# A Mamba and mixture-of-experts layer on one core: the places of all steps in a 64-slot timetable are renumbered

## What is computed

```python
x = L0_attn_x                                   # (8, 1024, 512)
xz = layernorm(x) @ in_proj_w.T                 # x_ssm and z
x_conv = silu(causal_conv4(x_ssm) + conv_b)
B, C, delta = split(x_conv @ x_proj_w.T)        # 16, 16 and 1 wide; softplus on delta
def step(h, inp):                               # scan over 1024 steps, state 512 x 16
    h = exp(dt * A) * h + dt * B * xt
    return h, (h * C).sum(-1)
y = (ys + D_param * x_conv) * silu(z)
x = x + y @ out_proj_w.T
p = softmax(layernorm(x) @ router_w.T + router_b)
w, idx = top_k(p, 2)                            # two of eight experts per token
x = x + sum_k w_k * (layernorm(x) @ expert_weights[idx_k])
```

## Time and profile before

| what | value |
|---|---|
| time, median of 3 runs | 2778.48 us (2769.5 to 2797.36) |
| profiled execution, its own time | 2768.58 us |
| its span, first to last instruction | 2766.5 us, mean granted clock 0.926 |
| busy of the span | PE 84%, DVE 82%, POOL 65%, ACT 54% |
| instructions | 34600 |

### The profile page before, as it was taken

How to read it: one execution, slowest core, us unless ns; L and a number is a source line. 1 busy time by engine, 2 the same in 40 slices (tenths; PEclk the granted TensorE clock), 3 DMA queues, 4 the chain that set the end, 5 groups by cost and what they waited for, 6 DMA issues and landing times.

```text
span 2766.5 us, 34600 instructions
## 1 busy us (share of the span) xinstructions
PE 2313.6 (84%) x9510; PEld 1336.4 (48%) x9510; DVE 2273.5 (82%) x3144; ACT 1488.8 (54%) x2417; POOL 1809.8 (65%) x1418
## 2 busy tenths in 40 slices
PE   5668777798979889798988889798987989798886
PEld 2435353554545454454545455454544545454432
DVE  3899999899899989898999979898899989888200
ACT  3554646465654746565564656556574656545221
POOL 2556767557576767768676766767686676669442
PEclk8878788799989999898999989899999999999998
DMA  3873412324233434435343444534444353456875
GB/s 121 277 264 95 155 59 58 96 77 134 73 122 112 138 118 116 132 111 145 114 146 103 123 132 109 145 104 148 115 121 128 105 155 107 126 153 183 217 209 152
DMA packets 192570, 366.27 MB, mean 132 GB/s; under 512 B 22912, under 2 KB 22912, under 8 KB 192384
## 3 DMA queue, kind: packets, MB, share of 16 engines
q1 hardware_dynamic: 144272, 263.26, 29.8%
q0 software_dynamic: 28672, 67.13, 11.3%
q10 hardware_dynamic: 19440, 33.69, 3.4%
HBM read 212.73 MB, written 151.26 MB: 132 GB/s over the span
## 4 chain that ended last, share of the span: by engine, by line
PE 33%; DVE 24%; POOL 15%; issue 14%; ACT 11%; DMA 2%; SPq 0%; DVEq 0%; POOLq 0%; another core or an unknown queue 0%; ACTq 0%
DVE h L1069 13%; PE bank L1240 12%; PE bank L1244 11%; POOL u L785 9%; PE bank L1255 7%; DVE acc L1077 6%; ACT bank L930 4%; PE bank L1235 3%; DVE xc L1100 2%; ACT L930 1%; ACT xc L982 1%; POOL row_scratch L872 1%; PE bank L1317 1%; POOL row_scratch L870 1%; POOL x_out L885 1%
## 5 line engine op out<-in xcount | busy, mean ns | idle before, releaser
L785 POOL TENSOR_TENSOR u<-xc,b_ring 128x1024 f32<-128x1024 f32 x512 | 1230.2, 2419 | 644.4 <-DVE h L1069 434.9
L930 ACT ACTIVATE bank<-dt,neg_a 128x512 f32<-128x512 f32 x1024 | 701.6, 689 | 799.4 <-DVE h L1069 686.4
L1255 PE MATMUL bank<-ident,h 128*128 128x128 f32 x4096 | 643.4, 292 | 240.5 <-DVE h L1069 137.5
L1255 PEld LDWEIGHTS bank<-ident,h 128*128 128x128 f32 x4096 | 511.2, 150 | 559.4 <-DVE h L1069 206.2
L1069 DVE TENSOR_TENSOR_SCAN h<-bank,h_last,u 128x512 f32<-128x512 f32 x512 | 652.7, 1276 | 93.8 <-ACT bank L930 52.6
L1077 DVE SCALAR_TENSOR_TENSOR acc<-bank,ct,acc 128x512 f32<-128x512 f32 x960 | 696.5, 726 | 7.7 <-PE bank L1255 7.5
L1069 DVE TENSOR_TENSOR_SCAN h<-bank,u 128x512 f32<-128x512 f32 x512 | 620.9, 1215 | 92.8 <-ACT bank L930 54.6
L1240 PE MATMUL bank<-w_exp,xeT 128*128 x764 | 381.6, 623 | 43.5 <-ACT xeT L1038 20.5
L1244 PE MATMUL bank<-w_exp,xeT 128*128 x764 | 362.1, 596 | 0.0
L1240 PE MATMUL bank<-xnT,w_in 128*128 128x512 f32 x512 | 257.4, 627 | 9.2 <-DVE acc L1077 3.6
L1244 PE MATMUL bank<-xnT,w_in 128*128 128x512 f32 x512 | 242.3, 596 | 0.0
(11 more groups left out here) (149 smaller groups left out, 2193.1 us busy)
## 6 DMA issues: line engine op xcount, KB each, us to landing
b_ring<-b_scratch SPq DMA_DIRECT2D x256, 256.0 KB
xe<-row_scratch SPq DMA_DIRECT2D x165, 256.0 KB
result_scratch<-ye SPq DMA_DIRECT2D x165, 256.0 KB
row_scratch<-x_out ACTq DMA_DIRECT2D x32, 1024.0 KB, 5.4
x<-in_x SPq DMA_DIRECT2D x66, 256.0 KB, 4.3
x_scratch<-x SPq DMA_DIRECT2D x64, 256.0 KB, 2.4
xn<-in_x SPq DMA_DIRECT2D x62, 256.0 KB, 3.7
x_out<-x_scratch SPq DMA_DIRECT2D x44, 256.0 KB, 4.6
```

The source lines that it names most:

```text
L785: nc.gpsimd.tensor_tensor(out=u[:, at:at + 2, :], in0=xc[:, half, 2 * k:2 * k + 2, :], in1=b_ring[:, n % ROWS:n % ROWS + 1, :].to_broadcas ...
L930: nc.scalar.activation(decay_bank(j, n, c)[:], dt[:, half, :], ACT.Exp, scale=neg_a[:, c, n:n + 1]).then_inc(decay_ready, 1)
L1255: last = nc.tensor.transpose(ps[:, k * P:(k + 1) * P], tile(k), ident[:])
```

## The change

It gives every step of every table a new place. The steps themselves, their waits, the buffers and the number of banks stay. The diff is a list of numbers from end to end, of which two lines show the kind:

```diff
     POST = {
-        "y_gate": [6.67, 6.71, 10.4, 10.55],
+        "y_gate": [8.48, 9.55, 10, 11.25],
...
     EXPERTS = {
-        "rows_evict": [11.12, 15.78, 21.27, 24.77, 30.71, 34.35, 36.91, 44.06, 46.66, 53.82, 62.38, 68.96],
+        "rows_evict": [12.15, 14.12, 22.01, 26.09, 30.02, 35.09, 37.8, 45.59, 50.98, 56.34, 61.83, 68.77],
```

More of the change, by code:

```diff
@@ L62, in mamba_moe_kernel @@
     COMBINE = {
-        "fetch": [3.46, 12.94, 35.73, 39.01],
-        "gather": [8.8, 12.29, 29.08, 31.46, 41.89, 47.71, 54.7, 60.67],
-        "store": [27.39, 35.74, 61.02, 66.51],
+        "fetch": [0, 14.07, 36.73, 39.67],
+        "gather": [15.46, 18.52, 31.63, 33.77, 40.96, 46.13, 55.24, 59.7],
+        "store": [28.21, 36.82, 59.92, 63.22],
     }
     POST = {
-        "load_res": [2.18, 3.07, 4, 5.1],
-        "y_T": [4.43, 4.52, 4.87, 4.87],
-        "y_skip": [5.75, 5.85, 7.57, 7.79],
@@ L82, in mamba_moe_kernel @@
-        "gate_top": [32.75],
-        "gate_exp": [35.51],
-        "gate_sum": [34.41],
-        "gate_weights": [37.72],
-        "rank": [35.14],
-        "row_of": [38.98],
-        "weigh": [40.93, 51.87, 56.55, 61.19],
-        "scatter": [48.38, 52.16, 59.82, 62.85],
+        "load_res": [1.53, 4.84, 4.9, 5.81],
+        "y_T": [4.87, 4.87, 4.93, 4.96],
+        "y_skip": [5.67, 6.6, 7.25, 8.34],
+        "y_gate": [8.48, 9.55, 10, 11.25],
+        "out_project": [10.88, 11.89, 13.76, 14.86],
@@ L90, in mamba_moe_kernel @@
+        "gate_sum": [36.3],
+        "gate_weights": [39.07],
+        "rank": [38.08],
+        "row_of": [39.96],
+        "weigh": [40.35, 51.87, 55.22, 60.86],
+        "scatter": [46.94, 53.76, 57.69, 64.06],
     }
     PREP = {
-        "load_x": [0, 0.96, 8, 8.36],
-        "norm_stat": [5.92, 7.34, 15.35, 15.62],
-        "norm_rstd": [10.21, 19.08],
-        "norm_apply": [10.01, 10.14, 18.01, 18.99],
-        "norm_T": [9.89, 9.9, 16.62, 17.49],
-        "norm_evict": [12.69, 15.17, 19.56, 20.09],
@@ L98, in mamba_moe_kernel @@
-        "project": [19.75, 22.85, 26.73, 30.64],
-        "project_end": [22.04, 23.15, 26.75, 31.81],
-        "z_project": [41.87, 44.86, 50.33, 55.86],
-        "z_project_end": [45.98, 46.69, 54.05, 56.94],
-        "conv_first": [24.92, 27.58, 31.32, 33.74],
-        "conv": [25.96, 26.63, 26.77, 29.89, 30.06, 30.69, 33.81, 34.1, 35.13, 35.88, 36.01, 36.4],
-        "conv_edge": [36.97],
-        "z_evict": [48.82, 49.67, 57.75, 60.86],
-        "silu_x": [38.14],
-        "silu_z": [62.14],
@@ new lines, in mamba_moe_kernel @@
+        "project": [20.3, 22.85, 26.73, 31],
+        "project_end": [22.04, 23.15, 26.75, 31.75],
+        "z_project": [42.47, 45.67, 51.05, 56.23],
+        "z_project_end": [44.78, 46.77, 54.45, 56.94],
+        "conv_first": [25.24, 28.35, 30.8, 36.1],
+        "conv": [24.62, 25.02, 25.89, 28.28, 29.17, 30.92, 32.48, 33.33, 34.17, 35.3, 35.9, 36.92],
+        "conv_edge": [37.92],
+        "z_evict": [49.01, 52.17, 58.3, 61.37],
+        "silu_x": [39.36],
+        "silu_z": [62.14],
+        "dt_project": [40.84],
@@ L122, in mamba_moe_kernel @@
[L122 to L125 removed]
+        "rows_T": [9.66, 11.88, 20.04, 23.29, 26.89, 32.15, 34.95, 40.47, 43.88, 50.77, 58.35, 65.77],
@@ L165, in mamba_moe_kernel @@
+        "end_rank": [49.38],
         "end_row_of": [66.9],
[L166 removed]
+        "end_weigh": [43.31, 47.48, 52.76, 54.69],
         "end_scatter": [66.9, 66.9, 66.9, 66.9],
```

141 lines of the change are left out of this document (72 added, 69 removed).

## The result

The changed kernel takes 2793.3 us (median of 20 runs), the kernel before 2769.4 (median of 20); the ratio is 1.0085, 95% interval 1.0072 to 1.0099. That is 24 us more, where 27.5 less was forecast.

What follows compares the result with a forecast made beforehand. No queue was full; PE set the pace in its chain, DVE's order elsewhere. Six even blocks -29.0, six odd -0.5, block 15 +2.0: -27.5 from 2778.5 gives 2751 us, own range 2735 to 2767, with rivals 2712 to 2803.

Steps and rivals of the forecast that it cites:

- PE's chain: From out_project 0 to project_end 0: rows_T leaves, -0.44 us; a wait of expert comes in, 0.7 even, 1.3 odd.
- single banks: Decays in the bank of the one before: 0.2 us each uncovered, +1.2 us in even blocks, +1.0 in odd.
- Behind the chain: After project_end 0: gate_weights gives -1.2 us even, -0.2 odd; one h_sum wait -0.6; load and two scans -0.4 together.
- The head of even blocks: Block start to out_project 0: expert_end and POOL work move out of the way, so the product comes 4.1 us earlier.
- The wait of `expert` for `rows_evict`: In PE's chain, rows_evict behind slot 22's decay makes expert wait: 0.7 us even, 1.3 odd, bounds 0 and 2.4.
- the clock: At out_project 0 of even blocks: a shorter wait could keep the upper level, a further 1.0 us each; counted as nothing.
- the four groups of waits: DVE's waits for decay, `u`, `y_T` and `h_T`: 99.4 us in ten blocks, called two thirds of its idle time.
- the slower one: Rival, chance 0.20: expert waits 2.4 us in every block and single banks cost in every slot; +31, 2809 us.
- three signs by which the prediction was to be known as wrong: out_project 0 to project_end 0 over 2 us longer; odd blocks falling like even; blocks 15 and 16 changing over 10 us.
- Absorbed: Rival, chance 0.20: the chain's start moves only by what expert_end gives, y_gate hands the delay on; -8, 2770 us.
- Block 15 and the end: Block 15 has ten more single-bank decays, +2.0 us; the end was put at 0, with 10 us either way.

Runs made afterwards that it cites:

- rank_psum: The changed kernel with the sum of rank and row_base written back into its PSUM bank, nothing else; ratio 1.0052 to the kernel before.
- after_banks: The changed kernel, with a decay not taking the bank of the decay before it if any other is idle; ratio 1.0231 to the kernel before.
- late49: The changed kernel with the places from 49 to 64 of the steady tables put back; ratio 1.0001 to the kernel before.
- after_scatter: The changed kernel with the third scatter alone put back from 57.69 to 59.82; ratio 1.0151 to the kernel before.
- zev49: The kernel before with one number changed, z_evict 0 from 48.82 to 49.01, its new place; ratio 1.0118 to the kernel before.
- late_before: The changed kernel with the places from 50 to 64 of the four steady tables put back; ratio 1.0116 to the kernel before.
- warm: The changed kernel with the first norm_T of each block from 3 on done six times over; ratio 1.0036 to the kernel before.
- head_only: The kernel before with the steady tables' new places where one of the two is under 19, and those past 64; ratio 1.0016.
- tail_before: The changed kernel with the four tables of block 15 and the end put back; ratio 1.0094 to the kernel before.
- mid: The kernel before with rank plus row_base kept in PSUM and only the new places between 36 and 47; ratio 1.0011.
- row39_psum: The kernel before with row_of moved from 38.98 to 39.96 and rank plus row_base kept in PSUM; ratio 1.0051.

## Why the prediction was wrong

The terms of the sum against the traces, us a block (from the third row on counted by the scans of slots 24, 48 and 64, which leaves 0.3 us of each block out):

| term | even, forecast | measured | odd, forecast | measured |
|---|---|---|---|---|
| head, to `out_project` 0 | -4.1 | -2.8 | -0.75 | -0.2 |
| PE's chain | +0.26 | +1.3 | +0.86 | -0.06 |
| behind it, the waits that go (slots 24 to 48) | -2.2 | -0.2 | -1.2 | -0.1 |
| behind it, slots 48 to 64 (single banks) | +1.2 | +2.1 | +1.0 | +2.0 |
| block | -4.8 | +0.74 | -0.1 | +1.96 |

Forecast and traces lie 52 us apart (-27.5 against +24.4). Over twelve blocks the third row is 19 of these, the fourth 11, the head 11; the two chains nearly cancel, and blocks 0 to 2 add 6.

- **The step that failed is "Behind the chain".** The prediction subtracted 1.2 and 0.2 for `gate_weights`, 0.6 for `h_sum` and 0.4 for small things as if nothing would come in their place. The waits did go, 2.3 us a block. But `row_of`, which moved too, had no term: beside a `u` one of its products takes 2.0 us instead of 0.19, and DVE's work in these slots rose by as much as its waits fell. That this is the port is shown for the product (rank_psum). What the kernel would be without the stall is not, because the edit passes it on to the cast; 9 us is what it gave with about half of the stall left. In slots 36 to 44 it takes 0.9 us of work off DVE, of which even blocks keep 0.5 and odd ones 0.1, the rest being a longer wait for the decay. Most of the 9 us come from blocks 1 to 4, where both products are slow and L1177 takes 4.4 us a block, against 2.2 to 2.3 in blocks 5 to 14.
- **POOL's order at the end of the block** had no term either; `scatter` is not in the prediction at all. It stands ahead of the `u` of slot 58 now, and the scans of slots 58 and 60 wait 1.4 us in even blocks and 1.2 in odd ones. In after_banks, which unties the decays, slots 56 to 60 stay as long (9.0 us), and in late49 the wait is gone. Put back alone, the scatter did worse (after_scatter), so the wait hangs on the crowding of scatter, gather and `u`, not on one place.
- **The single banks** had about the right size: 0.2 us for each tied decay that nothing covers, +1.2 and +1.0. In the change slots 48 to 56 lose 0.85 us a block, of which after_banks takes 0.7 back. What the prediction did not see is how high the price can go elsewhere: five tied decays cost 2.3 and 3.2 us a block in zev49, and untying them gives 2.8 and 2.4 in slots 48 to 60 (late49 against late_before). The 0.20 is that of a lone one; with one bank ACT can't run ahead, so the evictions, the `weigh`s and what POOL does behind a `weigh` come on DVE's path as well.
- **Where the loss lies** is shown by late49: with the places from 49 on put back the kernel takes 1.0001. So the new places from 49 on cost 23 us, and those ahead of 49 bring nothing as a whole, where all of the gain was forecast.
- **The head of even blocks**: the mechanism was right, the size 2.8 instead of 4.1. Up to `y_skip` 0 came 1.3 of the 1.72 of `expert_end`, and from there to `out_project` 0 1.4 of the 2.4 of POOL's moves; what held back the rest no run isolates.
- **PE's chain** grew by 1.3 in even blocks. The wait of `expert` for `rows_evict`, which I feared, was 0.29 and 0.35 us (0.7 and 1.3 forecast); the cost was the clock: in warm, with `out_project` 0 at the upper level, the chain takes 38.17 us, 2.0 less. The prediction counted nothing for the clock; the rule it quoted from the Trainium skill (TensorE: Matmul & The Clock Gate, Part 1: The HAM clock gate), that activity lifts the clock, agrees with warm, but idle time of 1.1 to 1.4 us was still there just ahead of the product, 3.44 us for 2.94. In odd blocks the clock went the other way. The prediction took 1.98 us from block 9; the mean of the six before was 2.72, and it is 1.98 now. That gain of 0.7 it had not counted, so that the odd chains stayed as long as they were was in part luck.
- **The readings**: the four groups of waits, 9.9 us a block, are 57% of the 17 us in which DVE does nothing, not two thirds.
- **The rivals**: the slower one came nearest in time (2809, or 2800 from the median of 20, against 2793), but by another way. Its `expert` wait of 2.4 wasn't there, and that its 2.2 and 1.8 us for the banks equal the loss behind slot 48 is chance, since about half of that is POOL's. Of the three signs by which the prediction was to be known as wrong none came. Absorbed let the chain's start stand still. In head_only it came 2.7 us earlier and the chain took most of that back: what absorbed forecast as a sum, by a way it did not name.
- **Block 15 and the end** moved by 3 us, inside the 10 allowed, and its tables don't matter (tail_before). Blocks 0 to 2 lost 5.8 us, of which rank_psum returns 3.1. Of the 3 us of block 0, 2.4 are there in mid too, and none in row39_psum or head_only: they come with the places from 36 to 47, and not with `row_of`.

## What to carry to other kernels

Where one list orders all queues, the buffers are handed out by the same list, so a step moved past one neighbour can change who shares a bank for a dozen slots: diff the hand-out, not only the order, and price a buffer that lost its double by all that stands between its uses, on the other queues too. A small operation is as costly as what it stands beside: look up for each moved DVE operation where its operands lie and what POOL runs then, compare its duration before and after, and after a repair look at its neighbours, to which the stall may have moved. Fewer waits in total (half the waits for decays here) say nothing, as long as it isn't known which of them PE's chain covered and whether the engine's own work grew instead.
